# Order of three loads on the sync engine in a mixture-of-experts loop: rows, gate and up weights, down weights becomes gate and up weights, down weights, rows

## The reference

```
scores = softmax(x @ wg_router.T);  topk_w, topk_idx = top_k(scores, 6)      # 32 experts, 1024 tokens
C = 2 * (T * 6 // 32)                                                         # 384 places for each expert
xe = zeros(32, C, 256).at[flat_idx, safe_pos].add(x_rep)                      # rows gathered by expert
g = einsum('ecd,edf->ecf', xe, w_gate);  u = einsum('ecd,edf->ecf', xe, w_up) # f = 176
ye = einsum('ecf,efd->ecd', silu(g) * u, w_down)
y = sum over k of ye[flat_idx, safe_pos] * topk_w                             # back to the tokens
return y + (silu(x @ ws_gate) * (x @ ws_up)) @ ws_down                        # and a shared expert
```

## Time and profile before

| | |
|---|---|
| median of 3 runs | 989.39 us |
| the profiled execution | 989.41 us |
| its span in the trace | 987.8 us |
| TensorE busy | 779.2 us, 79% |
| VectorE busy | 630.9 us, 64% |
| ScalarE busy | 505.6 us, 51% |
| GpSimd busy | 431.9 us, 44% |

### The profile page before, as it was taken

How to read it: one execution, slowest core, us unless ns; L and a number is a source line. 1 busy time by engine, 2 the same in 40 slices (tenths; PEclk the granted TensorE clock), 3 DMA queues, 4 the chain that set the end, 5 groups by cost and what they waited for, 6 DMA issues and landing times.

```text
span 987.8 us, 17657 instructions
## 1 busy us (share of the span) xinstructions
PE 779.2 (79%) x4548; PEld 663.9 (67%) x4548; DVE 630.9 (64%) x2152; ACT 505.6 (51%) x1274; POOL 431.9 (44%) x340
## 2 busy tenths in 40 slices
PE   5897837989898306789999999999878689988841
PEld 4465726888788204567887878788766688888830
DVE  3565624667667267689778788797465467776522
ACT  2332314667677322565565665556423477777621
POOL 2004773657666513123122132130647267667551
PEclk9997977999999659799999999999959799999955
DMA  9955736888798430000000000000234689889645
GB/s 351 426 208 198 259 125 187 210 203 224 195 228 186 91 107 1 1 1 1 1 1 1 2 1 1 1 17 1 107 118 142 196 217 229 215 217 227 147 90 167
DMA packets 65591, 130.85 MB, mean 132 GB/s; under 512 B 8388, under 2 KB 36420, under 8 KB 63872
## 3 DMA queue, kind: packets, MB, share of 16 engines
q1 hardware_dynamic: 41104, 93.77, 28.5%
q0 software_dynamic: 24432, 36.44, 17.6%
HBM read 75.25 MB, written 54.92 MB: 132 GB/s over the span
## 4 chain that ended last, share of the span: by engine, by line
PE 34%; DVE 18%; issue 15%; DMA 15%; POOL 8%; ACT 6%; SPq 1%; DVEq 1%; POOLq 1%; ACTq 1%
DMA raw<-in_w_gate_up 6%; PE bank L315 6%; POOL token_rows L1791 6%; PE bank L317 5%; PE bank L316 5%; DMA over<-token_rows 3%; PE bank L852 3%; PE bank L817 3%; DVE over L1670 2%; PE bank L841 2%; PE bank L650 2%; DVE halves L1498 2%; DVE over L1626 2%; DVE over L1632 2%; PE bank L558 2%
## 5 line engine op out<-in xcount | busy, mean ns | idle before, releaser
L315 PE MATMUL bank<-halves 88*128 88x256 f32 (+2 forms) x548 | 193.4, 353 | 32.0 <-DVE halves L1498 19.0
L317 PE MATMUL bank<-halves 88*128 88x256 f32 (+2 forms) x548 | 173.5, 317 | 0.0
L316 PE MATMUL bank<-halves 88*128 88x256 f32 (+2 forms) x548 | 173.3, 316 | 0.0
L315 PEld LDWEIGHTS bank<-halves 128*128 128x128 f32 (+1 forms) x548 | 108.8, 198 | 51.7 <-issue 41.1
L1791 POOL DMA_INDIRECT token_rows<-xn,slot_ids x96 | 98.8, 1030 | 101.8 <-issue 69.3
L316 PEld LDWEIGHTS bank<-halves 128*128 128x128 f32 (+1 forms) x548 | 109.9, 201 | 0.9
L317 PEld LDWEIGHTS bank<-halves 128*128 128x128 f32 (+1 forms) x548 | 108.6, 198 | 1.0
L1480 DVE TENSOR_TENSOR over<-over,bank 128x176 f32<-128x176 f32 x128 | 42.6, 333 | 72.8 <-ACT over L1026 72.3
L1893 POOL TENSOR_TENSOR over<-over 128x512 f32<-128x512 f32 x16 | 20.6, 1285 | 144.5 <-DVE over L1632 144.5
L1165 ACT ACTIVATE over<-over,nb,rqs 128x256 f32<-128x256 f32 (+1 forms) x128 | 71.7, 563 | 10.8 <-DVE nb L1658 10.8
L1002 ACT ACTIVATE halves<-raw 128x704 fp32r<-128x704 f32 x64 | 50.5, 790 | 50.5 <-DMA raw<-in_w_gate_up 47.1
(11 more groups left out here) (214 smaller groups left out, 2030.5 us busy)
## 6 DMA issues: line engine op xcount, KB each, us to landing
raw<-in_w_gate_up SPq DMA_DIRECT2D x64, 352.0 KB, 4.0
over<-token_rows SPq DMA_DIRECT2D x64, 320.0 KB, 3.4
token_rows<-over SPq DMA_DIRECT2D x10, 1536.0 KB, 21.1
raw<-in_w_down SPq DMA_DIRECT2D x64, 176.0 KB
over<-in_w_qkv_b SPq DMA_DIRECT2D x1, 4096.0 KB, 14.4
raw<-in_w_shared SPq DMA_DIRECT2D x6, 384.0 KB, 3.2
w_out_b_sb<-in_w_out_b SPq DMA_DIRECT2D x1, 2048.0 KB, 25.0
raw<-in_w_gate_up POOLq DMA_DIRECT2D x5, 352.0 KB, 4.4
```

What stands on the lines that cost most here:

```text
L315: nc.tensor.matmul(out, hi, rhs_lo, start=start, stop=False)
L316: nc.tensor.matmul(out, lo, rhs_hi, start=False, stop=False)
L317: return nc.tensor.matmul(out, hi, rhs_hi, start=False, stop=stop)
```

## The change

In both places of `expert_traffic` where SP loads for expert e + 2, `rows` now comes after `gate_up` and `down` instead of before them. Nothing else differs: the waits of each load, the sizes, the buffers and all other engines' programs are as before.

```diff
@@ -391,15 +391,15 @@
             sp.dma_start(sums[0][0:TOK, :].rearrange("(i p) d -> p i d", p=P), x_tok[:, :, :]) \
                 .then_inc(x_stored, 16)
             for e in range(2):
-                rows(e + 2, e)
                 gate_up(e + 2, e)
                 down(e + 2, e)
+                rows(e + 2, e)
             with sp.Fori(1, E // 2 - 1) as k:
                 for par in range(2):
                     e = 2 * k + par
-                    rows(e + 2, par)
                     gate_up(e + 2, par)
                     down(e + 2, par)
+                    rows(e + 2, par)
 
         def sums_back(sp, layer, sums):
```

## The result

Over 20 runs each, taken side by side, the changed kernel took 995.65 us in the median and the kernel before 989.88. The ratio is 1.0066, with a 95% interval of 1.0044 to 1.0089: slower, by two thirds of a per cent. A later comparison gave 1.0092 (1.0052 to 1.0132). Forecast were 973 us and a range of 962 to 991. By the bound of 2% it is no change, but the sign is clear and it is the other one.

A forecast was written before the change was run, and what follows sets the result against it. It took the expert loops as nearly balanced, held up by gate and up weights issued late behind the rows load. Gains of 10.8, 2.6, 1.5 and 1.9 us, together 16.8, took 989.4 to 973 us; range 962 to 991.

The forecast's parts named there:

- weights turn: Gate and up buffer, release to release in the expert loops: 9.5 us a pair before, 7.4 after, leaving the path.
- half clock stretches: TensorE's stretches at 1.2 GHz after pauses within the expert loops were to go; first-layer mean clock was 0.96.
- rows turn: Rows buffer, transposes to landing of the next load: 9.2 us a pair before, 9.6 after, 10.4 with the longest landing.
- prediction's own formula: Rows buffer's time per pair of experts: 6.15 us (5.42 + 0.63 + 0.1) plus the landing of the rows load.
- rival 1: Slower: rows land late behind the weights in the expert loops, 992 to 1020 us; chance 0.12.
- threshold of 3.97 us: Rows landing above which the rows turn passes the present pace in the second layer; 4.58 in the first.
- results turn: Result buffers, copy through scatter to next copy: 9.66 to 10.18 us, untouched by the change; 9.9 taken as pace afterwards.
- signs of being wrong: Line 650 waiting for `token_rows` in the loop, rows landing over 4.2 us in the median, or scatters landing later.
- first layer's 10.8: Gain in us from the first layer's loop: pace from 10.73 to 9.9 us a pair over 13 pairs.
- second layer's gain of 2.6: Gain in us from the second layer's loop: pace from 10.12 to 9.9 us a pair over 12 pairs.
- head's 1.5: Start of the first layer: expert 3's wait of 1.75 us mostly goes, gaining 1.5 us.
- tail's 1.9: End of the second layer: three experts take 14.9 us instead of 16.74, gaining 1.9 us.

The follow-up runs named there:

- small loads: Changed kernel, from expert 2 loading only 16 columns of down weights (0.9892 of before, not comparable) or of gate and up weights (0.9841); results wrong.
- second profile: The changed kernel run once more without any edit, for another profile: 1.0092 of the kernel before.
- own waits: Changed kernel, but each result tile waits only for its own scatter of two experts back, where the first waited for both: 1.0080 of before.
- rows in the middle: Changed kernel with the rows load moved between the gate and up load and the down load: 0.9992 of the kernel before, 985.59 us.
- early taking: VectorE takes gates and row numbers right behind its gate and up split, not its down split: on the kernel before 1.0096, on the changed kernel 1.0102.
- T: TensorE transposes the rows after turn_hidden instead of before: on the kernel before 1.0003, changed kernel 1.0045, rows in the middle 0.9922.
- W: Each result tile waits by its own semaphore for its own scatter: on the changed kernel 1.0080; on rows in the middle with T 0.9902.

## Why the prediction was wrong

**The weights turn** was right, step by step: ewlo is the last thing the load waits for, the issue follows in 0.2 us, and ScalarE's 24 us of waits went to zero, not merely under 5. The half clock stretches went with it (0.99 for 0.96 in the first layer). The fit of 2.0 us plus bytes at 436 GB/s, which I had set against this turn's 3.9 us, is given by the Trainium skill ("DMA: Bandwidth & Descriptors", Anatomy of one DMA) for DMAs that GpSimd issues. These loads are the sync engine's, so the measured landing does not decide against it.

**The rows turn failed, at its landing.** The issue came 0.34 us later, as worked out (0.4). For the landing I wrote "I take 3.4 to 4.2, nearest to the former", because the weights would mostly be through. It was 4.2, and 4.0 in the first layer, although the gate and up weights had a lead of 2.6 us in the median and not 1.9. The two kernels with small loads show that the weights' bytes make it: 3.6 without the down weights, 3.4 without the gate and up weights. With 4.2 the prediction's own formula, 6.15 + 4.2, gives 10.35 us a pair, and 10.27 stands in the timeline.

**This is rival 1**, which I had given 0.12, and 995.65 us lies in its span (992 to 1020). Its threshold of 3.97 us was passed in the second layer, which became 0.39 us a pair slower. The one of 4.58 in the first layer was not passed, and there the formula fails too: 6.15 + 4.0 gives 10.15 us a pair, and measured were 10.62 and, in the second profile, 10.74. Read over the whole first loop, the mean turn is 5.59 us from the transposes to the taking, 0.66 to the issue and 4.38 from there to the transposes two experts on. Against the formula that is 0.17 and 0.03 more for the first two, and 0.28 more for the landing with its wake: I had used one expert's turn and a median landing, and the pace is a mean over experts that land after 3.2 to 5.2 us. The rival's price was set at a landing of 5.0, which never was the median.

**The results turn** was taken as the pace afterwards with "The change does not touch it". It does. From the second scatter to the copy it was 5.8 us in the median for 5.3 before, one of the prediction's own signs of being wrong; with the 4.52 of the earlier trace rows that is 10.3 us a pair, not 9.9. So the rows turn and the results turn both came out longer than the pace that I had forecast. Only the rows turn cost time: without its waits for scatters the changed kernel keeps its paces (10.72 and 10.55) and its time (1.0080).

**Sum.** Of the forecast 16.8 us, the first layer's 10.8 shrank to 13 x 0.11 = 1.4 (to nothing in the second profile, 10.74 for 10.73), and the second layer's gain of 2.6 became a loss of 12 x 0.39 = 4.7. The head's 1.5 did not come: from the first rows load to that of expert 4 are 17.78 us before (148.44 to 166.22) and 17.80 after. Of the tail's 1.9 came 1.0 (914.80 to 930.51 is 15.71 us, for 16.74). Loops alone give about +3 us in these two profiles, where the medians differ by 5.8. From expert 31's rows load to the end of the span are 64.2 us before and 59.6 in the changed kernel (59.1 in its second profile), a gain that stands in no term; with one profile of the kernel before it can't be told from scatter. What makes up the rest is open: the profile of the changed kernel was one of its faster executions.

**What is shown and what is argued.** Shown: that rows hold the changed kernel and waits for scatters do not (own waits); that moving rows ahead of down gives the loss back (rows in the middle); that the weights' bytes lengthen the landing (small loads). Argued only: that it is their place in the queue, and that the sum of the DMA traffic is what keeps all versions above 9.6 us a pair. The kernel with 344 KB fewer for each expert is faster, which fits the latter, but it also changes when the rows land, and in the first layer it makes no better than 10.23 with the DMA engines busy 0.75 of the time.

**The best version** found issues gate and up weights, rows, down weights, or keeps the old order with the early taking, and adds T and W: 0.9902 and 0.9886 of the kernel before, about 1%. They beat both kernels; between them, and the first of them without W (0.9922), the runs don't decide.

## What to carry to other kernels

Where several double buffers share one issuing queue, write down each buffer's turn, release to release, with the landing of its load in it; a change of order shortens one turn by the wait it is spared and lengthens another by its place in the queue and by the bytes ahead, and the next longest turn has only the difference as its room. With DMA engines already busy 0.9 of the time, an early load is not free. Price the landing of what comes behind it higher: here 528 KB ahead added 0.8 us, between nothing and the 2.1 us that all of them would take at 250 GB/s. And look at transfers of other queues that the early load will fall upon. Take means over all experts for a turn, not one expert. No new order of the three loads was faster by itself than the old one (rows in the middle 0.9992, rows last 1.0066); time was gained only when the engines' own order or waits were moved with it.

## What was not expected of the hardware

- A load of 320 KB that landed after 3.4 us when issued first of three took 4.2 us behind 528 KB issued 0.5 and 2.7 us ahead of it. As an estimate, 2.7 us at the loop's 250 GB/s are 675 KB, more than the 352 KB that had this lead. It made hardly a difference whether the last 176 KB were issued 0.5 us ahead of it or behind it (4.0 and 3.9 us in the first layer).
- A transfer of another queue took longer with loads behind it than with loads ahead of it: a scatter of 128 rows of 1 KB let its waiter go after 5.3 us in the median (4.8 to 6.4) with all three loads issued ahead of it, after 5.8 with the gate and up weights behind it, and after 6.3 us (5.4 to 6.9) with rows and these weights issued about 1.1 and 1.6 us behind it.
- ScalarE's waits for scatters could be cut from 34 to 3 us in 145 us of the loop with the time hardly changed (0.9922 to 0.9902): the wait moved to the rows.
